# Top-2 routing of a mixture of experts by wide comparisons over several chunks, in place of 8-element maximum and index instructions for each chunk

## The reference

```python
x = x + conv3x3(fake_quant(ln_over_channels(x)), fake_quant(conv_w))
t = to_tokens(x)                       # 8192 tokens of 64 channels
xf = ln_over_channels(t)
logits = xf @ gate_w + gate_b          # 8 experts
probs = softmax(logits)
top2_vals, top2_idx = top_k(probs, 2)
cw = zeros(N, 8).at[arange(N)[:, None], top2_idx].add(top2_vals)
for e in range(8):
    acc += cw[:, e, None] * (gelu(xf @ W1[e] + b1[e]) @ W2[e] + b2[e])
x = from_tokens(t + acc)
```

## Time and profile before

| | us |
|---|---|
| median of 3 runs | 225.83 (225.80 to 226.24) |
| span of the profiled execution | 223.9 |
| the same with what lies around it, by the median | 225.8 (1.9 around) |
| PE busy | 181.7 (81% of the span), 955 matmuls |
| DVE busy | 144.0 (64%), 456 instructions |
| ACT busy | 116.9 (52%) |
| POOL busy | 124.7 (56%) |
| mean granted TensorE clock | 0.910 of full |

### The profile page before, as it was taken

The page is one execution under the profiler, slowest core; times in us unless marked ns, Lnnn a source line. Parts: engine busy times, 40 slices in busy tenths (PEclk is TensorE's granted clock), DMA queues, the critical chain, the costliest instruction groups (busy, mean ns, idle before and its releaser), DMA issues.

```text
span 223.9 us, 3616 instructions
## 1 busy us (share of the span) xinstructions
PE 181.7 (81%) x955; PEld 71.6 (32%) x955; DVE 144.0 (64%) x456; ACT 116.9 (52%) x153; POOL 124.7 (56%) x118
## 2 busy tenths in 40 slices
PE   3975206950499829799999999999999999999990
PEld 3954202530166824342222222222222222222220
DVE  0999999009977799649666476376466475433352
ACT  2459500334025857446965656665666655666550
POOL 7695008600694426136775666666566666666663
PEclk9999555995579976999999999999999999999997
DMA  6930000000000003956939549449469399089201
GB/s 196 301 47 3 0 1 0 1 1 0 0 0 3 0 0 92 197 101 176 199 96 207 129 124 207 104 126 199 104 153 203 71 218 203 27 188 190 68 3 47
DMA packets 16174, 22.32 MB, mean 100 GB/s; under 512 B 2202, under 2 KB 7970, under 8 KB 16162
## 3 DMA queue, kind: packets, MB, share of 16 engines
q1 hardware_dynamic: 16002, 22.04, 43.9%
q10 hardware_dynamic: 160, 0.15, 0.2%
HBM read 19.82 MB, written 2.36 MB: 99 GB/s over the span
## 4 chain that ended last, share of the span: by engine, by line
PE 62%; DVE 20%; issue 6%; ACT 5%; POOL 2%; DMA 2%; POOLq 1%; DVEq 0%; ACTq 0%
PE ps L1069 26%; PE ps L1054 25%; PE ps L985 7%; DVE xn L630 3%; DVE ssum L618 3%; DMA cw<-in_conv_w 2%; POOL qpad L355 1%; DVE gbc L693 1%; ACT hl L493 1%; DVE topi L807 1%; PE ps L942 1%; ACT work L546 1%; DVE xn L697 1%; ACT work L422 1%; DVE xn L716 1%
## 5 line engine op out<-in xcount | busy, mean ns | idle before, releaser
L403 POOL TENSOR_TENSOR x<-x,y_sb 128x512 f32 (+1 forms) x63 | 80.2, 1273 | 51.2 <-DVE y_sb L846 50.7
L546 ACT ACTIVATE work<-ps,bias_sb,w_back 128x1024 f32<-128x1024 f32 x64 | 76.9, 1204 | 48.8 <-PE ps L1054 48.7
L846 DVE SCALAR_TENSOR_TENSOR y_sb<-ps,bias_sb,gbc 128x512 f32<-128x512 f32 x64 | 47.9, 750 | 52.4 <-PE ps L1069 42.8
L1069 PE MATMUL ps<-work,w_sb 128*64 128x512 f32 x256 | 68.8, 617 | 0.3 <-DVE y_sb L846 0.3
L1054 PE MATMUL ps<-xT,w_hi 128*128 (+1 forms) x128 | 39.5, 391 | 0.1
L1054 PE MATMUL ps<-xT,w_lo 128*128 (+1 forms) x128 | 38.9, 386 | 0.0
L985 PE MATMUL ps<-qpad,cw_bd 128*128 128x512 bf16 x72 | 21.1, 452 | 21.5 <-POOL qpad L355 21.5
L1069 PEld LDWEIGHTS ps<-work,w_sb 128*64 128x64 f32 x256 | 12.8, 134 | 28.1 <-issue 23.5
L1054 PEld LDWEIGHTS ps<-xT,w_hi 128*128 128x128 f16 x128 | 8.3, 100 | 41.8 <-issue 41.4
L355 POOL TENSOR_TENSOR qpad<-work,xn 128x512 bf16<-128x512 f32 (+1 forms) x8 | 11.4, 1436 | 14.7 <-issue 7.5
L985 PEld LDWEIGHTS ps<-qpad,cw_bd 128*128 128x128 bf16 x72 | 7.7, 109 | 32.3 <-issue 15.5
(11 more groups left out here) (106 smaller groups left out, 178.5 us busy)
## 6 DMA issues: line engine op xcount, KB each, us to landing
gbc<-gate_rows SPq DMA_DIRECT2D x16, 768.0 KB, 9.9
gbc<-gate_rows SPq DMA_DIRECT2D x16, 256.0 KB, 3.9
x_sb<-in_x SPq DMA_DIRECT2D x8, 256.0 KB, 4.9
out<-x SPq DMA_DIRECT2D x8, 256.0 KB, 10.1
w_raw<-in_W SPq DMA_DIRECT2D x2, 256.0 KB, 5.8
w_sb<-in_W SPq DMA_DIRECT2D x1, 256.0 KB
gate_rows<-gateT SPq DMA_DIRECT2D x8, 32.0 KB, 1.9
cw<-in_conv_w ACTq DMA_DIRECT2D x2, 72.0 KB, 3.6
```

The source lines that it names most:

```text
L403: pool.tensor_tensor(x2[:, ds(c * W, W)], x2[:, ds(c * W, W)], y_sb[:, u % H_RING, :], ALU.add).then_inc(added, 1)
L546: act.activation(h_sb[:, u % H_RING, :], bank(H + 2 * (u % 2), 2 * W), ACT.Gelu, bias=b1_sb[:, u:u + 1], scale=w_back[:, u:u + 1]).then_in ...
L846: dve.scalar_tensor_tensor(y_sb[:, u % H_RING, :], bank(Y + u % 2), b2_sb[:, u:u + 1], gbc[:, slot, u, :], ALU.add, ALU.mult).then_inc(wei ...
L1069: last = pe.matmul(ps[r * CH:(r + 1) * CH, (Y + u % 2) * W:(Y + u % 2 + 1) * W], w2_sb[:, u, :], h_sb[:, u % H_RING, r * W:(r + 1) * W], s ...
```

## The change

The copy, the MAX8 and FIND_INDEX8 instructions and the u32 indices are gone. A whole part of the logits (two, two and four chunks, so 16, 16 and 32 groups) is handled at once by `select_part`. `leftmost_of_best` marks where the values equal their maximum, multiplies the marks with a rank (8 for expert 0 down to 1 for expert 7), takes the largest rank, and marks the one expert that has it. The first maximum is the one that `shifted_logits` already has. For the second, the first choice is pushed down by -3e38 and the maximum taken again. `sum_part` sums the exponentials, inverts the sums and multiplies the exponentials with the two marks; `gates(c)` does the last product for a chunk. Every step waits for the one before it (`link`, now without `base`, as `mark` and `settled` are gone). select_part(0), sum_part(0) and gates(0) stand behind high_half(4); gates(1) behind normalise(7); select_part(1) and sum_part(1) between take_xT(5) and take_xT(6); select_part(2) behind unit 5 of chunk 0; sum_part(2) behind unit 1 of chunk 1. In the loop only gates(c + 2) is left, behind unit 4. The new tiles are hit, rest, best, sel1, sel2 (32 groups each), and sel, esum, rsum for all chunks; their declarations are left out here.

```diff
@@ -41,6 +41,7 @@
 BELOW_4_3 = 1.33333325386047363281
 AMAX_FLOOR = 1e-30
 WSCALE = 2.0 ** 13
+NEVER = -3.0e38
 
 E2M1_MIDS = (5.0, 3.5, 2.5, 1.75, 1.25, 0.75, 0.25)
 
@@ -320,8 +321,8 @@
                                     base=0, pattern=[[-1, CH]], channel_multiplier=1))
             pool.affine_select(out=stack_id[:, :], in_=stack_id[:, :], fill=1.0, compare_op=ALU.not_equal,
                                base=-CH, pattern=[[-1, CH]], channel_multiplier=1).then_inc(const_ready, 1)
-            link(pool.iota(iota_i[:, :, :], pattern=[[0, GROUPS], [1, EXPERTS]], base=0, channel_multiplier=0))
-            pool.tensor_copy(iota_e[:, :, :], iota_i[:, :, :]).then_inc(const_ready, 1)
+            link(pool.iota(iota_i[:, :], pattern=[[-1, EXPERTS]], base=EXPERTS, channel_multiplier=0))
+            pool.tensor_copy(rank[:, :], iota_i[:, :]).then_inc(const_ready, 1)
             pool.memset(cw_bd[:, :, :, :].rearrange("p a b c -> p (a b c)").bitcast(fp32), 0.0)
             pool.memset(cw_x[:, :, :, :, :].rearrange("p a b c d -> p (a b c d)").bitcast(fp32),
                         0.0).then_inc(cwx_zero, 1)
@@ -792,46 +777,48 @@
                                   m.unsqueeze(2).to_broadcast([128, n, EXPERTS]), ALU.subtract).then_inc(z_ready, 1)
 
 
-            def route_copy(c):
-                mark(dve.tensor_copy(lcur[:, :, :], logit[:, ds(c, 1), :, :].rearrange("p z g e -> p (z g) e")))
-
-            def route_max(groups):
-                settled(stand=True)
-                for g in groups:
-                    last = dve.max(top[:, g, :], lcur[:, g, :])
-                mark(last)
-
-            def route_index(groups):
-                settled(stand=True)
-                for g in groups:
-                    last = dve.max_index(topi[:, g, :], top[:, g, :], lcur[:, g, :])
-                mark(last)
-
-            wide_e = lambda a: a.to_broadcast([128, GROUPS, EXPERTS])
-
-            def ex_of(c):
-                return ex[:, ds(c, 1), :, :].rearrange("p z g e -> p (z g) e")
-
-            def route_sum(c):
-
-                dve.wait_ge(exp_ready, 1 + (c // 2 if isinstance(c, int) and c < EARLY else 2))
-                dve.tensor_reduce(esum[:, :], ex_of(c), AX.X, ALU.add)
-
-            def route_select():
-                settled()
-                dve.tensor_tensor(sel1[:, :, :], iota_e[:, :, :], wide_e(topi[:, :, 0:1]), ALU.is_equal)
-                mark(dve.tensor_tensor(sel2[:, :, :], iota_e[:, :, :], wide_e(topi[:, :, 1:2]), ALU.is_equal))
-
-            def route_gates(c):
-                settled()
-                dve.reciprocal(rsum[:, :], esum[:, :])
-                link(dve.tensor_tensor(sel[:, :, :], sel1[:, :, :], sel2[:, :, :], ALU.add))
-                link(dve.tensor_tensor(picked[:, :, :], ex_of(c), sel[:, :, :], ALU.mult))
+            def part_of(t, k):
+                first, last = LOGIT_PARTS[k]
+                return t[:, first:last, :, :].rearrange("p z g e -> p (z g) e")
+
+            def leftmost_of_best(k, values, chosen, own):
+
+                n = (LOGIT_PARTS[k][1] - LOGIT_PARTS[k][0]) * GROUPS
+                over_e = lambda a: a.unsqueeze(2).to_broadcast([128, n, EXPERTS])
+                ranks = rank[:, :].unsqueeze(1).to_broadcast([128, n, EXPERTS])
+                link(dve.tensor_tensor(hit[:, 0:n, :], values, over_e(own), ALU.is_equal))
+                link(dve.tensor_tensor(hit[:, 0:n, :], hit[:, 0:n, :], ranks, ALU.mult))
+                link(dve.tensor_reduce(best[:, 0:n], hit[:, 0:n, :], AX.X, ALU.max))
+                link(dve.tensor_tensor(chosen[:, 0:n, :], over_e(best[:, 0:n]), ranks, ALU.is_equal))
+
+            def select_part(k):
+
+                first, last = LOGIT_PARTS[k]
+                n = (last - first) * GROUPS
+                l = part_of(logit, k)
+                leftmost_of_best(k, l, sel1, lmax[:, first:last, :].rearrange("p z g -> p (z g)"))
+                link(dve.scalar_tensor_tensor(rest[:, 0:n, :], sel1[:, 0:n, :], NEVER, l, ALU.mult, ALU.add))
+                link(dve.tensor_reduce(best[:, 0:n], rest[:, 0:n, :], AX.X, ALU.max))
+                leftmost_of_best(k, rest[:, 0:n, :], sel2, best[:, 0:n])
+                link(dve.tensor_tensor(part_of(sel, k), sel1[:, 0:n, :], sel2[:, 0:n, :], ALU.add))
+
+            def sum_part(k):
+
+                first, last = LOGIT_PARTS[k]
+                dve.wait_ge(exp_ready, k + 1)
+                e = esum[:, first:last, :].rearrange("p z g -> p (z g)")
+                link(dve.tensor_reduce(e, part_of(ex, k), AX.X, ALU.add))
+                dve.reciprocal(rsum[:, first:last, :].rearrange("p z g -> p (z g)"), e)
+                link(dve.tensor_tensor(part_of(sel, k), part_of(ex, k), part_of(sel, k), ALU.mult))
+
+            def gates(c):
                 if not (isinstance(c, int) and c == 0):
 
                     dve.wait_ge(gateT_done, c)
-                dve.tensor_tensor(gate[:, :, :].rearrange("p e g -> p g e"), picked[:, :, :],
-                                  wide_e(rsum[:, :].unsqueeze(2)), ALU.mult).then_inc(gate_ready, 1)
+                dve.tensor_tensor(gate[:, :, :].rearrange("p e g -> p g e"),
+                                  sel[:, ds(c, 1), :, :].rearrange("p z g e -> p (z g) e"),
+                                  rsum[:, ds(c, 1), :].rearrange("p z g -> p (z g)").unsqueeze(2)
+                                  .to_broadcast([128, GROUPS, EXPERTS]), ALU.mult).then_inc(gate_ready, 1)
 
             def weigh(c, u, slot, times):
                 n = UNITS * c + u
@@ -852,19 +839,14 @@
                     if first and u == 0:
                         take_xT(NCH - 1)
 
-                    if route and u == 0:
-                        route_copy(c + 2)
-                        route_sum(c + 2)
-                    if route and u == 1:
-                        route_max(range(GROUPS))
-                    if route and u == 2:
-                        route_index(range(GROUPS))
-                    if route and u == 3:
-                        route_select()
+                    if route and u == 4:
+                        gates(c + 2)
                     if first and u == 3:
                         shifted_logits(2)
-                    if route and u == 4:
-                        route_gates(c + 2)
+                    if first and u == 5:
+                        select_part(2)
+                    if isinstance(c, int) and c == 1 and u == 1:
+                        sum_part(2)
 
 
             reduce_squares(2, sq2, ss2)
@@ -884,44 +866,31 @@
             reduce_squares(7, sq2, ss2)
             dve.wait_ge(gb_ready, 1)
             shifted_logits(0)
-            settled()
-            route_copy(0)
             invert(LN2_PARTS, 2, std2, rstd2)
-            route_max(range(GROUPS))
             normalise(4, LN2_PARTS, rstd2, xn2_ready)
-            route_index(range(GROUPS))
             high_half(4)
-            route_sum(0)
-            route_select()
+            select_part(0)
+            sum_part(0)
+            gates(0)
             normalise(5, LN2_PARTS, rstd2, xn2_ready)
-            route_gates(0)
             high_half(5)
             normalise(6, LN2_PARTS, rstd2, xn2_ready)
             shifted_logits(1)
             high_half(6)
             normalise(7, LN2_PARTS, rstd2, xn2_ready)
-            settled()
-            route_copy(1)
+            gates(1)
             high_half(7)
             take_xT(4)
-            route_max(range(GROUPS))
             take_xT(5)
-            route_index(range(GROUPS))
-            route_sum(1)
-            route_select()
-            route_gates(1)
+            select_part(1)
+            sum_part(1)
             take_xT(6)
-            PER = 6
             ffn(0, 0, 1, first=True)
             ffn(1, 1, 1)
 
-            start = count[0]
             with dve.Fori(1, (NCH - 2) // 2) as i:
-                base[0], count[0] = (i - 1) * (2 * PER) + start, 0
                 for s in range(2):
                     ffn(2 * i + s, s, i + 1)
-                assert count[0] == 2 * PER, count[0]
-            base[0], count[0] = 0, start + 2 * PER * ((NCH - 2) // 2 - 1)
             for s in range(2):
                 ffn(NCH - 2 + s, s, NCH // 2, route=False)
 
```

More of the change, by code:

```diff
@@ L86, in program @@
         ex = sb("ex", [128, NCH, GROUPS, EXPERTS])
-        lcur = sb("lcur", [128, GROUPS, EXPERTS])
-        top = sb("top", [128, GROUPS, 8])
-        topi = sb("topi", [128, GROUPS, 8], u32)
-        esum = sb("esum", [128, GROUPS])
-        rsum = sb("rsum", [128, GROUPS])
-        sel1 = sb("sel1", [128, GROUPS, EXPERTS])
-        sel2 = sb("sel2", [128, GROUPS, EXPERTS])
-        sel = sb("sel", [128, GROUPS, EXPERTS])
-        picked = sb("picked", [128, GROUPS, EXPERTS])
+        PART = 4 * GROUPS
+        hit = sb("hit", [128, PART, EXPERTS])
+        rest = sb("rest", [128, PART, EXPERTS])
+        best = sb("best", [128, PART])
+        sel1 = sb("sel1", [128, PART, EXPERTS])
```

(8 more changed lines are left out.)

16 lines of the change are left out of this document (2 added, 14 removed).

## The result

The changed kernel takes 231.03 us (median of 5 runs, 230.36 to 232.39) against 225.80 us (5 runs, 225.09 to 226.24): 2.5% slower, ratio 1.0246, 95% interval 1.0212 to 1.0280. That is +5.2 us, where +3.7 us were forecast; the direction and the range (227.2 to 232.0) hold. The trace shown is of an execution of 230.6 us span (232.39 us, the slowest of the five).

A forecast was written before the change was run, and what follows sets the result against it. TensorE sets the pace in the experts' chunks, but at 78 to 112 us VectorE's unbroken work is waited for. Early +1.5 us and the second selection's +2.2 us make +3.7, so 225.8 becomes 229.5 us; range 227.2 to 232.0.

The forecast's parts named there:

- Price of one step: VectorE's selection: each dependent step costs 0.32 us on 128x128 and 0.45 us on 128x256.
- Step 1: VectorE before the first gate: selection plus a POOL stall delay chunk 0's gate +1.5 us, the second shifted_logits' result +2.2.
- Step 2: Before the first unit: chunk 1's cheap gate offsets the late first gelu, then select_part(1) delays second product 2 by +1.5 us.
- the late clock: TensorE's half clock before the first unit may last up to one product longer, +0.7 us, counted only in the range.
- The balance with the DMA path: Gate rows for the third weighting also come +1.5 us late, at 102.05 us; this and second product 2's delay hide each other.
- Step 3: select_part(2) behind unit 5 delays unit 6's weighting; second product 8 stands 1.8 to 2.7 us, middle 2.2.
- Step 4: Later expert chunks: sum_part(2) costs nothing, and the removed 2.85 us a chunk is only free time on VectorE.
- the case that I gave 0.48: The main forecast, +3.7 us to 229.5 us, within 228.3 to 230.6 us.
- the first rival, the falling clock: TensorE's clock falls in the new pause before second product 8, 1.8 us more, 231.3 us; chance 0.22.

The follow-up runs named there:

- as_changed: The changed kernel run once more with no edit, beside the variants: 232.08 us against 225.84 us for the kernel before.
- The two failed moves: On the changed kernel, gates(1) moved behind take_xT(5) (232.01 us), or high_half(4) moved behind the first selection, sum and gate (231.32 us).
- fill: Changed kernel with eight extra unread matmuls on TensorE in the pause before second product 8, chunk 1 written out ahead of the loop: 230.14 us.
- spread: Changed kernel with select_part(2) in eight pieces behind units 5 to 13 and sum_part(2) moved behind unit 6 of chunk 1: 227.43 us.
- gate1_moved: Changed kernel with gates(1) moved from in front of high_half(7) to behind take_xT(5): 232.01 us, ratio 1.0283 to the kernel before.
- select_first: Changed kernel with select_part(0), sum_part(0) and gates(0) in front of high_half(4) instead of behind it: 231.32 us, ratio 1.0252 to the kernel before.
- before_parts3: Kernel before with the broadcast gate rows in three parts instead of two: 225.10 us, ratio 0.9976.
- neither: Chunks 0 and 1 routed as in the kernel before, chunks 2 to 7 by the wide selection with its steps spread: 226.95 us, ratio 1.0056.
- warm_short: Changed kernel with 4-step selection (no tie rule), gates(1) behind take_xT(5), gate rows in three parts, and filler matmuls in early TensorE pauses: 223.64 us.

## Why the prediction was right, and where its sizes were off

**Price of one step.** Right: 0.32 and 0.455 us measured, 0.32 and 0.45 taken, from the rows that waited in the same way.

**Step 1.** Right: +1.46 us at the first gate, forecast +1.5; the fourth step stood 0.81 us in place of 0.29 (forecast 0.66 late, measured 0.52); the second shifted_logits' result 2.2 us late, as forecast.

**Step 2** was mis-sized: +1.5 forecast, 2.3 to 2.6 measured. "take_xT(5) runs then", 90.5 us, is 13.1 us behind the first shifted_logits; it ran at 13.8 (after) and 14.1 (as_changed). The term is the gate of chunk 1, put down at 0.15 us; in the trace after the next operation started 0.99 us behind it. The trace of before has the row that I should have read, a copy in the same place, between normalise(7) and high_half(7), and take_xT(5) behind it:

```profile
86.01 1.15 POOL L382 TENSOR_TENSOR hl<-xn,hl  x1 [0.84 <-DVE hl L769]
...
86.18 1.03 DVE L796 COPY lcur<-logit 128x64 f32<-128x64 f32 x1
...
88.93 0.69 DVE L776 COPY xT<-ps 128x1024 f16<-128x1024 f16 x1 [0.24 <-PE ps L1012]
```

The copy cost 0.95 us there, so the gate's stall is no new loss against the kernel before: the place costs what it did, where the forecast had it 0.8 us shorter. take_xT(5) came 11.57 us behind the first shifted_logits before and 13.80 after: the 2.2 us of Step 1 arrive in full. The two failed moves show that the stall is not the gate's own price but the low halves', which find another operation wherever the gate stands.

In the traces of as_changed, fill, spread, gate1_moved and select_first something else comes on top: TensorE's half clock, over at 10.9 us behind the first shifted_logits in the trace after, lasts to between 13.3 and 14.2, and take_xT(5) waits for TensorE until 13.85 to 14.26. That is the late clock that the forecast had in its range at up to 0.7 us; second product 2 stands 0.1 to 0.5 us later in these traces than in the trace after. It also took up the 0.17 us that gate1_moved had won at take_xT(4). The balance with the DMA path did not hold either. The third weighting, which waits for the gate rows, came 23.19 us behind the first shifted_logits before, and between 22.99 (as_changed) and 25.27 (fill) in the traces with the late first gate, but second product 4 followed second product 2 by 5.56 us in all of them.

**Step 3.** Right in place and size: a pause ended by the weighting of unit 6, 1.93 us measured, 1.8 to 2.7 forecast; in the positions 2.0 us against the middle of 2.2. One stall of 0.95 us instead of 1.1 to 1.5. The 0.44 us for a gelu ahead of the pause is no part of the loss: before_parts3 has it too.

**Step 4.** Right: the 82 us above, with 14 us less VectorE and the same TensorE.

**The chances** were the weak place. The range held, but the case that I gave 0.48 did not: 231.03 us lies above its 228.3 to 230.6. The case that happened is the first rival, the falling clock, at 231.3 us and 0.22; I priced it at 1.8 us and it costs 1.6. That its time came within 0.3 us of the median is partly luck, as its sum had the early loss 0.8 us or more too small and the pause and the clock 0.2 us too large each. The forecast reasoned that the new pause lies between one of 1.3 us that left the clock alone and one of 2.6 that did not. Its own middle, 2.2 us, lay nearer to the second, so the rows spoke at least as much for the rival as against it; measured were 0.44 and 1.93 us with one product between. The sum of the measured terms (2.3 to 2.6, 2.0, 1.6) is 5.9 to 6.2 in the traces, and the medians differ by 5.2 and 6.2.

## What to carry to other kernels

Ask of a replacement not how many instructions or microseconds it takes off an engine, but how many dependent steps it puts in front of the first thing that others wait for: 11 wide steps for two chunks were longer than one chunk's eight-wide instructions, and the first gate needs only one chunk. Wide steps for chunk 0 alone were not tried. Work for later chunks that is put in one piece into an in-order engine stands before everything behind it; in small pieces the same work was free of the 2 us pause and of the clock's fall. And a pause of the matmul engine has two prices, its length and what the clock takes afterwards.

## What the runs showed of the hardware that I had not expected

**A stall for POOL is not tied to an instruction.** Removed from one VectorE operation (0.85 us from the gate, 0.52 us from a selection step) it came back both times at a cast from SBUF, which took 1.15 us instead of 0.41 and 0.43. The forecast had named only two-input operations; the copy of chunk 1's logits in the trace of before (86.18, above), next to a low half of POOL, already showed it for one input.

The Trainium skill (SBUF — State Buffer, Who interferes with whom) counts copies and casts in their fast modes with the operations that take the shared ports; the casts at 1.15 us agree.

**A fall of the clock by a pause of 2 us.** In five of five traces a pause of 1.93 to 2.44 us, 0.44 us and a product earlier another, was followed by a stretch at half clock; pauses of 1.3 to 1.5 us (before, after, neither) never were. The lengths don't simply add up: warm_short has pauses of 1.59 and 1.25 us, ending at 84.83 and 87.55 us of its trace, together more than the 0.44 and 1.93 of the trace after, and its clock stays at 1.00. What decides between the two these runs don't show.

**The noise lies in front of the changed stage.** The first shifted_logits started between 75.30 and 78.77 us in the traces, with nothing changed ahead of it but constants written at the start. In the convolution the clock rises at a different moment: in the same stretch its mean was 0.97 before (first line) and 0.66 after (second).

```profile
40.00:42.00 2.00, 2.00 (x10) 0.82 (x9) 0.00 (x0) 0.31 (x1) 1.55 (x2) 0.97 0.00 0
```

```profile
40.00:42.00 2.00, 2.00 (x7) 0.72 (x6) 0.00 (x0) 0.16 (x1) 1.69 (x2) 0.66 0.00 0
```

Up to 75 us the clock was low for some 24 us in spread (start at 75.30), 31 in before and after (77.36 and 78.13) and 34 in neither (78.77). Over the traces the later starts mostly go with more time at half clock, but not to the tenth of a us, and no run changed it on purpose. It is the likely reason why the medians of like kernels differ by more than the stages do. Positions behind a common point told the runs apart where the times did not.
